# Mixer B's chunk loop: decay applied after the state product, and six step products in one fp32 pass

## The reference, cut to what matters

```python
def step(h, inp):
    dt_t, x_t, B_t, C_t = inp
    dA = jnp.exp(dt_t * A)
    h = h * dA[..., None, None] + jnp.einsum('bh,bhp,bn->bhpn', dt_t, x_t, B_t)
    y_t = jnp.einsum('bhpn,bn->bhp', h, C_t)
    return (h, y_t)
...
y = jnp.moveaxis(yT, 0, 1) + D[None, None, :, None] * xs
y = rmsnorm(y.reshape(b, l, D_INNER) * jax.nn.silu(z), ssm_norm_w)
return y @ out_proj_w.T
```

## Time and profile before

| | us |
|---|---|
| three runs | 1003.5, 1005.3, 1012.17 |
| the profiled execution | 999.77 |
| its span, first to last instruction | 997.5 |
| busy PE / DVE / ACT / POOL | 952.9 / 723.2 / 570.0 / 616.1 |
| the same from 600 to 664, about the chunk loop | 62.07 / 50.84 / 52.90 / 51.88 |
| granted clock, mean of the span and from 600 to 664 | 0.988 and 1.00 |

### The profile page before, as it was taken

One profiled execution on the slowest core, in us unless ns is written; L12 is line 12 of the kernel. 1 busy time (PEld: TensorE's weight loads), 2 busy tenths in 40 slices (PEclk: granted clock), 3 DMA queues, 4 the chain that ended last, 5 costly groups with the idle time before them and its releaser, 6 DMA issues. The chain is left out here.

```text
span 997.5 us, 16126 instructions
## 1 busy us (share of the span) xinstructions
PE 952.9 (96%) x4711; PEld 676.6 (68%) x4711; DVE 723.2 (73%) x1192; ACT 570.0 (57%) x1046; POOL 616.1 (62%) x482
## 2 busy tenths in 40 slices
PE   7989999888899999999999999999999999999997
PEld 3323333233467799999998556766667999999996
DVE  3999998999588666665665797775597566566656
ACT  6764655665442555555554788787623555555553
POOL 1599897999531966965531397852306777567432
PEclk9999999998999999999999999999999999999999
DMA  5233223453341133322001300000702222420104
GB/s 159 67 75 84 75 78 73 93 113 89 103 137 46 43 91 92 77 77 81 31 28 42 110 1 1 2 1 1 226 0 75 73 83 64 118 72 28 33 24 133
DMA packets 69247, 69.70 MB, mean 70 GB/s; under 512 B 14952, under 2 KB 51568, under 8 KB 69168
## 3 DMA queue, kind: packets, MB, share of 16 engines
q1 hardware_dynamic: 64176, 58.44, 20.6%
q0 software_dynamic: 4992, 10.23, 3.9%
HBM read 58.00 MB, written 10.62 MB: 69 GB/s over the span
## 5 line engine op out<-in xcount | busy, mean ns | idle before, releaser
L810 POOL TENSOR_TENSOR a_hc<-a_h,a_c_sb 128x512 f32<-128x512 f32 x128 | 159.6, 1271 | 45.4 <-DVE a_h L711 45.3
L492 PE MATMUL ps<-a_hc,eye 128*128 128x512 f32 x256 | 133.1, 633 | 14.2 <-POOL a_hc L810 13.4
L629 ACT ACTIVATE ps<-a_delta,a_neg_a 128x512 f32<-128x512 f32 x128 | 87.0, 689 | 75.0 <-DVE a_h L711 72.4
L492 PEld LDWEIGHTS ps<-a_hc,eye 128*128 128x128 f32 x256 | 44.9, 194 | 81.9 <-POOL a_hc L810 45.1
L711 DVE TENSOR_TENSOR_SCAN a_h<-ps,a_state,a_b_u 128x512 f32<-128x512 f32 x64 | 78.6, 1265 | 1.8 <-ACT ps L629 1.4
L1214 PE MATMUL ps<-g_ring_rounded,g_q_hi_rounded 128*128 x312 | 77.1, 337 | 0.0
L1214 PE MATMUL ps<-f_ring_rounded,f_q_hi_rounded 128*128 x312 | 77.0, 337 | 0.0
L711 DVE TENSOR_TENSOR_SCAN a_h<-ps,a_b_u 128x512 f32<-128x512 f32 x64 | 75.0, 1205 | 1.9 <-ACT ps L629 1.7
L1067 POOL DMA_INDIRECT g_rows<-xn_rows,g_source x39 | 37.2, 954 | 58.8 <-DVE g_source L1700 38.1
L1067 POOL DMA_INDIRECT f_rows<-xn_rows,f_source x39 | 37.3, 957 | 54.6 <-DVE f_source L1700 35.5
L1078 POOL DMA_INDIRECT token_rows<-f_rows,f_back x39 | 37.9, 972 | 49.6 <-DVE f_rows L1752 26.9
(11 more groups left out here) (485 smaller groups left out, 2753.3 us busy)
## 6 DMA issues: line engine op xcount, KB each, us to landing
a_c_sb<-c_rows SPq DMA_DIRECT2D x64, 256.0 KB, 3.4
f_ring<-in_gu SPq DMA_DIRECT2D x16, 469.0 KB, 4.4
g_ring<-in_gu SPq DMA_DIRECT2D x16, 469.0 KB, 4.6
f_ring<-in_dn SPq DMA_DIRECT2D x8, 512.0 KB, 6.0
g_ring<-in_dn SPq DMA_DIRECT2D x8, 512.0 KB, 6.6
xn_rows<-f_work SPq DMA_DIRECT2D x8, 256.0 KB, 4.2
f_rows<-token_rows SPq DMA_DIRECT2D x8, 256.0 KB, 4.7
xn_rows<-g_work SPq DMA_DIRECT2D x8, 256.0 KB, 3.2
```

What stands on the lines that cost most here:

```text
L492: nc.tensor.matmul(ps[:, Y + f, :], k.eye[:, :], hc[:, s % WAITING, :], start=False, stop=(n == NST - 1)).then_inc(y_added, 1)
L629: nc.scalar.activation(ps[:, A + m % NA, :], delta[:, f, cols(g)], ACT.Exp, scale=neg_a[:, f, n:n + 1])\
L810: nc.gpsimd.tensor_tensor(hc[:, m % WAITING, :], h[:, s % DEPTH, :], c_sb[:, i % RING, :], ALU.mult)\
```

## The change

1. E is gone: its two matmuls, its exponential and `c_in`. The state product takes C as it is, once for each half of the channels (2 heads, 128 columns) instead of once per head, into a bank of its own (`INTER`), and not at all in the first chunk of a sequence. Since the decay from the chunk's start depends on token and head only, it multiplies the result: `take_inter` (DVE, once per pair) multiplies the bank by `of_decays`, and `gate_y` adds that into Y's bank.
2. The decays stand as one row per head and chunk (64 rows of 128), from a third product in `ends` and a third exponential. SP stores them to DRAM and loads them back spread over 64 partitions each, in four groups of four chunks, two loads of 256 KB per group, into `shifted`, whose work for the convolution is over by then.
3. In chunks 3, 5, 6, 8, 9 and 10 POOL makes `steps` once, unsplit, and D is one fp32 matmul.
4. The first state of a sequence is copied instead of added to zeros; one `keep` per sequence falls away.

The diff, cut: the counting of semaphores, the new layout of `dta` (by half, so that one array serves both uses) and unchanged lines between are left out.

```diff
+    k.decay_rows = nc.dram_tensor("decay_rows", (HEADS_B * TT, P), F32, kind="Internal").ap()
...
+    steps_whole, steps_hi = k.twin("b_steps_hi", [P, 2, HEADS, P], stage)
-    mix, c_in = [sb(n, [P, 2, HEADS, P]) for n in ("mix", "c_in")]
+    mix = sb("mix", [P, 2, HEADS, P])
+    decays_of = sb("decays_of", [HEADS * TT, P])
+    from_state = sb("from_state", [P, FT, 2, P])
...
-    Y, S, M, D, F, E, TR = 0, 2, 3, 4, 5, 6, 7
+    Y, S, M, D, F, INTER, TR = 0, 2, 3, 4, 5, 6, 7
+    WHOLE_STEPS = (3, 5, 6, 8, 9, 10)
+    GROUP = CH // P
...
+    def of_decays(g):
+        return shifted[:, g % 2, :].rearrange("p (f t) -> p f t", f=FT)
+
+    def chunks_of(v, g):
+        return v[:, :, (1 if 2 * g % PER_SEQ == 0 else 0):, :]
...
+            sp.wait_ge(rows_ready, 1)
+            sp.dma_start(k.decay_rows, decays_of[:, :]).then_inc(rows_moved, 16)
+            sp.wait_ge(rows_moved, 16)
+            half = HEADS * TT // 2
+            for g in range(NCH):
+                if g == 0:
+                    sp.wait_ge(pool_conv, 2 * (TAPS - 1))
+                else:
+                    sp.wait_ge(rows_moved, 16 + 32 * g)
+                if g >= 2:
+                    sp.wait_ge(inter_read, (g - 1) * GROUP // PAIR)
+                for q in range(2):
+                    rows = k.decay_rows[q * half:(q + 1) * half, :].rearrange("(f t) m -> f (t m)", f=FT)
+                    sp.dma_start(of_decays(g)[q * HD:(q + 1) * HD, :, :], rows[:, cols(g)].partition_broadcast(HD))\
+                        .then_inc(rows_moved, 16)
...
+                n = HEADS * TT
+                nc.tensor.matmul(ps[0:n, M, 2 * n:2 * n + P], dta[:, :, :, :].rearrange("p q f t -> p (q f t)"),
+                                 k.masks[:, 0, :], start=True, stop=True).then_inc(ends_ready, 1)
+
+            def of_steps(out, c):
+                if c in WHOLE_STEPS:
+                    return nc.tensor.matmul(out, k.masks[:, 1, :], steps_whole[:, c % 2, :, :].rearrange("p h i -> p (h i)"),
+                                            start=True, stop=True)
+                nc.tensor.matmul(out, later[:, :], steps_hi[:, c % 2, :, :].rearrange("p h i -> p (h i)"),
                                  start=True, stop=False)
-                return nc.tensor.matmul(out, which, steps_lo[:, c % 2, :, :].rearrange("p h i -> p (h i)"),
+                return nc.tensor.matmul(out, later[:, :], steps_lo[:, c % 2, :, :].rearrange("p h i -> p (h i)"),
                                         start=False, stop=True)
...
-                pe.wait_ge(steps_ready, 2 * c + 2)
+                pe.wait_ge(steps_ready, steps_of(c))
...
-                of_steps(ps[:, D, :], later[:, :], c).then_inc(d_ready, 1)
+                of_steps(ps[:, D, :], c).then_inc(d_ready, 1)
...
-                if c >= 1:
-                    pe.wait_ge(c_in_ready, c)
-                of_steps(ps[:, E, :], one[:, :], c).then_inc(e_ready, 1)
...
-                pe.wait_ge(c_in_ready, c + 1)
-                pe.wait_ge(state_ready, c + 1)
                 for h in range(HEADS):
                     a = h // 2 * PAIR * P + c % PAIR * P
-                    out = ps[HD * (h % 2):HD * (h % 2) + HD, Y + g % 2, a:a + P]
-                    nc.tensor.matmul(out, x_dt[:, c % 2, h, :], mix[:, c % 2, h, :], start=True, stop=False)
-                    last = nc.tensor.matmul(out, state[:, c % 2, h, :], c_in[:, c % 2, h, :], start=False, stop=True)
+                    last = nc.tensor.matmul(ps[HD * (h % 2):HD * (h % 2) + HD, Y + g % 2, a:a + P], x_dt[:, c % 2, h, :],
+                                            mix[:, c % 2, h, :], start=True, stop=True)
+                if c % PER_SEQ:
+                    pe.wait_ge(state_ready, states_of(c))
+                    if g:
+                        pe.wait_ge(inter_read, g)
+                    for f in range(FT):
+                        a = f * PAIR * P + c % PAIR * P
+                        last = nc.tensor.matmul(ps[:, INTER, a:a + P],
+                                                state[:, c % 2, 2 * f:2 * f + 2, :].rearrange("p h q -> p (h q)"),
+                                                cT[:, c * P:(c + 1) * P], start=True, stop=True)
                 last.then_inc(y_summed, 1)
...
-                act.wait_ge(e_ready, c + 1)
-                nc.scalar.activation(ps[:, E, :], ps[:, E, :], ACT.Exp).then_inc(into_ready, 1)
...
+            act.wait_ge(ends_ready, 3)
+            nc.scalar.activation(flat(e_end), ps[:, M, 0:n], ACT.Exp).then_inc(ends_done, 1)
+            nc.scalar.activation(flat(dt_end), ps[:, M, n:2 * n], ACT.Exp).then_inc(ends_done, 1)
+            nc.scalar.activation(decays_of[:, :], ps[0:n, M, 2 * n:2 * n + P], ACT.Exp).then_inc(rows_ready, 1)
             for c in range(TT):
                 chunk(c)
-                if c % PER_SEQ:
+                if c % PER_SEQ > 1:
...
-                    pool.wait_ge(e_ready, c - 1)
+                    pool.wait_ge(d_ready, c - 1)
+                if c in WHOLE_STEPS:
+                    shape = [P, FT, 2, P]
+                    nc.gpsimd.tensor_tensor(steps_whole[:, c % 2, :, :].rearrange("p (f q) i -> p f q i", f=FT),
+                                            k.masks[:, 0, :].unsqueeze(1).unsqueeze(1).to_broadcast(shape),
+                                            dta_by_head[:, c, :, :].unsqueeze(3).to_broadcast(shape),
+                                            ALU.mult).then_inc(steps_ready, 1)
+                    return
...
-                dve.wait_ge(into_ready, c + 1)
-                nc.vector.tensor_tensor(c_in[:, c % 2, :, :], ps[:, E, :].rearrange("p (h i) -> p h i", h=HEADS),
-                                        cT[:, ts].unsqueeze(1).to_broadcast([P, HEADS, P]), ALU.mult)\
-                    .then_inc(c_in_ready, 1)
...
+                if c % PER_SEQ == 0:
+                    return
...
-                if c % PER_SEQ == 0:
+                if c % PER_SEQ == 1:
                     dve.wait_ge(ds_ready, c)
-                    nc.vector.memset(state[:, c % 2, :, :], 0.0).then_inc(state_ready, 1)
+                    nc.vector.tensor_copy(state[:, c % 2, :, :],
+                                          ps[:, S, 0:HEADS * HD].rearrange("p (h q) -> p h q", h=HEADS))\
+                        .then_inc(state_ready, 1)
...
+            def take_inter(g):
+                dve.wait_ge(y_summed, PAIR * (g + 1))
+                n = g * PAIR // GROUP
+                dve.wait_ge(rows_moved, 16 + 32 * (n + 1))
+                a = g * PAIR % GROUP * P
+                decay = of_decays(n)[:, :, a:a + PAIR * P].rearrange("p f (c m) -> p f c m", c=PAIR)
+                nc.vector.tensor_tensor(chunks_of(from_state, g), chunks_of(in_pair(INTER), g), chunks_of(decay, g), ALU.mult)\
+                    .then_inc(inter_read, 1)
...
-                dve.wait_ge(yd_ready, (g + 1) * FT)
+                dve.wait_ge(inter_read, g + 1)
+                dve.wait_ge(yd_ready, g * (FT + 1) + FT)
+                y_now = chunks_of(in_pair(Y + g % 2), g)
+                nc.vector.tensor_tensor(y_now, y_now, chunks_of(from_state, g), ALU.add).then_inc(yd_ready, 1)
+                dve.wait_ge(yd_ready, (g + 1) * (FT + 1))
...
-            nc.vector.memset(state[:, 0, :, :], 0.0).then_inc(state_ready, 1)
...
+                if c % PAIR:
+                    take_inter(c // PAIR)
```

More of the change, by code:

```diff
@@ L37 @@
 TT = T // P
+HEADS_B = 4
 TILES = NI + 1
@@ L1875, in mixer_b_stage @@
     sem = lambda name: k.sem("b_" + name)
-    HEADS, HD = 4, 64
+    HEADS, HD = HEADS_B, 64
     MT = 3
@@ L1888, in mixer_b_stage @@
     shifted = sb("shifted", [P, 2, SEQ])
-    dt, dt_log, dta, dt_end, e_end = [sb(n, [P, TT, HEADS]) for n in "dt dt_log dta dt_end e_end".split()]
+    dt, dt_log, dt_end, e_end = [sb(n, [P, TT, HEADS]) for n in "dt dt_log dt_end e_end".split()]
+    dta = sb("dta", [P, 2, FT, TT])
+    dta_by_head = dta[:, :, :, :].rearrange("p q f t -> p t f q")
     dta_hi, dta_lo = [sb(n, [P, TT, HEADS], F32R) for n in ("dta_hi", "dta_lo")]
@@ L1892, in mixer_b_stage @@
     one, later = [sb(n, [P, P], F32R) for n in ("one", "later")]
-    steps_hi, steps_lo = [sb(n, [P, 2, HEADS, P], F32R) for n in ("steps_hi", "steps_lo")]
+    steps_whole, steps_hi = k.twin("b_steps_hi", [P, 2, HEADS, P], stage)
+    steps_lo = sb("steps_lo", [P, 2, HEADS, P], F32R)
     toks = sb("toks", [P, 2, 3 * P])
     gram = sb("gram", [P, 2, P])
-    mix, c_in = [sb(n, [P, 2, HEADS, P]) for n in ("mix", "c_in")]
+    mix = sb("mix", [P, 2, HEADS, P])
+    decays_of = sb("decays_of", [HEADS * TT, P])
+    from_state = sb("from_state", [P, FT, 2, P])
     x_dt, x_end, state = [sb(n, [P, 2, HEADS, HD]) for n in ("x_dt", "x_end", "state")]
@@ L1974, in part_of_x, with in_pair, steps_of, states_of @@
         return x_split[:, part, cols(c)]
+    def of_decays(g):
+        return shifted[:, g % 2, :].rearrange("p (f t) -> p f t", f=FT)
+    def chunks_of(v, g):
```

(33 more changed lines are left out.)

17 lines of the change are left out of this document (5 added, 12 removed).

## The result

The kernel after took 1009.44 us in the median (1004.68 to 1013.71, 20 runs) against 1005.61 (1002.62 to 1012.17, 20 runs) on the same chip: a ratio of 1.0038, 95% interval 1.0022 to 1.0055, within 1% and slower by 3.8 us where 0.6 less was forecast. The profiled execution took 1009.65 us (span 1007.1, mean clock 0.979; 0.988 before).

What follows compares the result with a forecast made beforehand. VectorE, in order and with bursts without waits, was taken to limit the gain, though TensorE is 96% busy. Loop -1.9 us and tail +1.3 summed to -0.6: 1004.7 us against a median of 1005.3, range 999 to 1009.5.

Steps and rivals of the forecast that it cites:

- the loop: Mixer B's chunk loop up to Y(15): Y(15) at about 659.2 instead of 661.08, -1.9 us.
- the tail: After Y(15), without cover: take_inter(7) and the add go in ahead of the last gated product, 0.61 + 0.72 = +1.3 us.
- DVE's work: Mixer B's loop on DVE: c_in removed -9.6, takes and adds +9.6; unchanged to 0.3 us, only moved towards the gating bursts.
- The add: DVE's add into Y, once per pair, priced as a dependent operation at 0.72 us, about 0.45 for pairs 0 and 4.
- PE's relief: PE alone in mixer B's loop: E's removal, whole D products and waits sum to -6.6 us.
- Rival A: Mixer B's loop: PE paces after all and DVE's waits shrink, -5.3 us at the bound, 1000.0 us; chance 0.25.
- the walk: Stage-by-stage account of mixer B's loop and what follows Y(15), following DVE's bursts and waits; sum -0.6 us.
- step 2: From D(6) to D(10): PE stalls of about 0.7, 0.6, 0.7 and 1.0 us in DVE's bursts; D(10) about 635.0 against 635.77.
- the whole D: D as one fp32 product in six chunks: 0.86 against 0.55 us on PE, 1.7 us from its start to DVE's mix.
- step 1: Loop up to gram(5): DVE loses five c_in (-3.0), gets takes and adds (+2.1); D(6) at about 618.7 against 619.31.
- step 3: Third and fourth groups of chunks repeat the second, pair 4 half-sized (-0.5), no whole D after chunk 10 (twice 0.3).
- Rival B: First pair: take(0) waits for decay rows landing after 608.2; +3.1 us at worst, about +1.5 typically; chance 0.15.

Runs made afterwards that it cites:

- no_add: Kernel after without DVE's add of the state's contribution into Y; ratio to the kernel before 0.9975, mix(3) to last gated product 49.86 us.
- after_filled: Kernel after with the skips of pairs 0, 2 and 4 moved between a gram and its mix; ratio to the kernel before 0.9993.
- all_split: Kernel after with no whole step products, D split in all 16 chunks; ratio to the kernel before 1.0013.
- rows_alone: Kernel before plus the third product, third exponential, store and eight loads of the decay rows, which nothing reads; ratio to the kernel before 1.0017.
- no_rows: Kernel after without the decay rows' store and loads, take_inter multiplying by `sz` in SBUF; ratio to the kernel before 1.0030.

## Why the prediction was wrong

The forecast was -0.6 us from the loop (-1.9) and the tail (+1.3). In the order of its steps, measured from the first gram (the forecast's steps also hold 0.15 us for the third exponential, which lies ahead of it):

| | forecast | measured |
|---|---|---|
| D(6) | -0.6 | 627.03 - 609.40 = 17.63 against 17.92: -0.29 |
| D(10) | -0.8 | 644.10 - 609.40 = 34.70 against 34.38: +0.32 |
| Y(15) | -1.9 | 59.36 against 59.69: -0.33 |
| Y(15) to the last gated product | +1.3 | 3.81 against 2.41: +1.40 |
| sum | -0.6 | +1.07 |

**Right.** DVE's work did not change (50.22 against 50.8 forecast within 1), and the loop without its waits went from 51.5 to 51.7: `c_in` came back as take and add. The add was priced 0.08 too low, as said. That PE's relief does not set the time is shown by the whole: 3.9 us less PE, 1.07 us more time. The tail was right to 0.1. Rival A (PE paces, -5.3 us) is refuted.

**The step that failed is the walk's credit for `c_in` in the chunks in which DVE waits**, above all in step 2, from D(6) to D(10), which was to bring 0.2 us and cost 0.61. The forecast had a zero sum of DVE's work and a shorter loop, so it needed shorter waits. They grew by 0.9 us, from 10.6 to 11.5. Step 2, piece by piece: from D(6)'s start to mix(6) +0.34 (1.41 to 1.75, the whole D, as the walk had it), then to mix(7) -0.51, to mix(8) +0.64, to mix(9) +0.61, and to D(10) -0.47 (1.31 to 0.84).

Two things held the gains down. First, D has one bank, so a chunk can't be shorter than the way from one mix to the next D (0.83, as from 626.20 to 627.03) and on to the next mix (1.36, or 1.75 for a whole D): 2.19 or 2.58 us. From mix(5) to mix(6) the kernel before was there already, at 2.25 without a wait; there the loss of `c_in` turned into 1.03 us of waiting, and the whole D lengthened the step. Steps that had been longer than that did get shorter: mix(9) to mix(10) from 3.08 to 2.59, with D(10) 0.84 instead of 1.31 us after mix(9), as PE has less to do ahead of it; mix(6) to mix(7) from 4.62 to 4.11; mix(13) to mix(14) from 2.95 to 2.54. Second, in the bursts nothing absorbs the take and the add. There the walk was nearly right in the rows (3.98 us from the state's sum to gram(8), 3.9 forecast), but it left out that the state's sum itself would wait 0.43 us longer.

`no_add` and `after_filled` show the same by experiment: the add in a burst is paid in full, and two of three pairs of skips, moved into waits, are free. A sum of DVE's work that is zero says nothing when what leaves lies ahead of waits and what comes lies in a row without one.

**Steps 1 and 3, and the whole D's price.** Of the -1.9 at Y(15), 1.6 were missing: 0.3 in step 1, 0.8 in step 2, and in step 3, which repeats it, 0.65 came of 1.1. In step 1 chunk 0's `c_in` won nothing (2.19 and 2.20 us from mix(0) to mix(1), with 0.37 and 0.97 us of waiting). A whole D takes 1.75 us to its mix, near the 1.7 of the walk, and together the whole steps behind mix(3) cost 0.73 (`all_split`); the walk charged 0.2 for D(3), and let the credits of `c_in` cover the others, which they do not.

**Rival B**, take(0) waiting for the decay rows, happened, at 0.52 us instead of the 0.9 of slack: the loads took 616.69 - 611.12 = 5.6 us from issue to the end of the wait, where the median of the nearest row gave 3.9 with the second issue. The Trainium skill's formula (DMA: Bandwidth & Descriptors, "Anatomy of one DMA") had been sooner still, 606.8 against 607.3 in the kernel before's time; by the trace it would have been about 608.7. That section fits its formula to transfers that GpSimd issues, and these are issued by SP. The wait stands ahead of mix(3), in the part of the loop that the change won, and `rows_alone` and `no_rows` show no trace of it behind that.

**PE** gave back 3.9 us where 6.6 were counted. The difference wasn't taken apart, as no term of the sum rested on it.

**The 2.7 us outside mixer B** were no part of any step. The interval of the copy of the kernel before includes a difference of that size, with no cause in the change; it stays open whether some of it is the kernel's.

Left open too: a second bank for D should cut the way from mix to mix. It wasn't tried, as all eight PSUM banks are in use in the loop.

## What to carry to other kernels

Where an engine waits in some stretches of a loop and never in others, price an operation by its place: count it in full in a row without a wait, and at nothing ahead of a wait whose end it does not move. Before adding work behind the last product of a group, look for the wait nearest by and put work there; here that order alone was worth some 2.7 us, half of what the adds cost. Give each stretch its own ruler, since medians over a whole kernel can't tell 1 us, and put no mark of the ruler between the place that an operation leaves and the one it goes to.
